# A four-layer attention and feed-forward kernel: a new order table, explicit waits for reused buffers, and a second buffer of reciprocal sums

## The reference, cut to what matters

```python
x = x + L0_xattn(ln(x), ctx, ctx)        # strict causal mask
x = x + ln(x) @ sign(W).T
x = x + L1_xattn(ln(x), ctx, ctx)        # causal mask
x = x + mixture(ln(x))                   # 16 experts, top 2, and 2 shared experts
x = x + L2_xattn(ctx, ln(x), mask)       # layer norms on q, k, v; a mask that is loaded
x = x + bitlinear_ffn(ln(x))             # 256 -> 1024 -> 256, weights rounded to -1, 0, 1
x = x + L3_xattn(ln(x), ctx, ctx)        # no weights, no mask
x = x + three_blocks(ln(x))              # low-rank corrected weights, layer norm, gelu
```

## Time and profile before

| | |
|---|---|
| median of 3 runs | 1159.62 us (1158.08 to 1163.7) |
| profiled execution, first to last instruction | 1166.1 us; the page gives no other time for it |
| PE, DVE, ACT, POOL busy | 90%, 78%, 69%, 48% |
| mean granted TensorE clock | 0.970 of full |
| moved by DMA | 140.03 MB, mean 120 GB/s |

### The profile page before, as it was taken

The page is one execution under the profiler, slowest core; times in us unless marked ns, Lnnn a source line. Parts: engine busy times, 40 slices in busy tenths (PEclk is TensorE's granted clock), DMA queues, the critical chain, the costliest instruction groups (busy, mean ns, idle before and its releaser), DMA issues.

```text
span 1166.1 us, 26103 instructions
## 1 busy us (share of the span) xinstructions
PE 1050.5 (90%) x8259; PEld 782.0 (67%) x8298; DVE 903.8 (78%) x3323; ACT 804.5 (69%) x1484; POOL 564.1 (48%) x1161
## 2 busy tenths in 40 slices
PE   7989999999999989898888898788898989989986
PEld 6667877777887866676666765556665665656664
DVE  3879887877564688898885588999997889887643
ACT  5757666566674555566565667656989899998962
POOL 7232364655122365577830125766455454545443
PEclk9999999999999998999999999979999999999997
DMA  7985322325667643412258864232132222222000
GB/s 239 312 284 143 92 74 56 91 74 173 203 181 210 200 127 82 136 47 84 81 185 262 249 184 147 84 92 76 39 100 73 73 55 56 83 64 55 1 19 19
DMA packets 102327, 140.03 MB, mean 120 GB/s; under 512 B 12336, under 2 KB 79792, under 8 KB 102192
## 3 DMA queue, kind: packets, MB, share of 16 engines
q1 hardware_dynamic: 98688, 129.57, 38.0%
q0 software_dynamic: 3072, 8.39, 2.3%
q10 hardware_dynamic: 432, 0.39, 0.1%
HBM read 65.43 MB, written 22.54 MB: 75 GB/s over the span
## 4 chain that ended last, share of the span: by engine, by line
PE 40%; DVE 18%; ACT 15%; DMA 8%; issue 7%; SPq 5%; POOL 5%; another core or an unknown queue 1%; DVEq 0%; POOLq 0%; ACTq 0%
PE ps L1559 9%; PE ps L1688 4%; ACT probs L2010 4%; PE ps L1580 4%; PE ps L1598 4%; SPq L2890 3%; PE ps L1781 3%; PE ps L1552 3%; PE ps L1566 2%; ACT q_st L2027 2%; DVE ps L2247 2%; DMA w<-in_expert 2%; PE ps L1601 2%; DVE ps L2255 2%; PE ps L1748 1%
## 5 line engine op out<-in xcount | busy, mean ns | idle before, releaser
L2010 ACT ACTIVATE probs<-ps 128x384 f32<-128x384 f32 (+1 forms) x512 | 260.2, 545 | 91.4 <-PE ps L1601 46.4
L1580 PE MATMUL ps<-k_st,q_st 96*128 96x256 bf16 (+1 forms) x1024 | 172.4, 266 | 26.8 <-DVE neg_max L2247 10.3
L1598 PE MATMUL ps<-q_st,k_st 104*128 104x256 bf16 (+1 forms) x1024 | 178.0, 263 | 16.8 <-ACT probs L2010 12.3
L2027 ACT ACTIVATE q_st<-ps 8x1024 bf16<-8x1024 f32 x128 | 129.9, 1016 | 24.4 <-PE ps L1669 21.8
L1580 PEld LDWEIGHTS ps<-k_st,q_st 96*128 96x128 bf16 x1024 | 86.8, 100 | 79.1 <-DVE neg_max L2247 19.1
L2247 DVE CUSTOM_DVE_ANT_0 ps<-ps,diag_s 128x128 f32<-128x128 f32 (+1 forms) x384 | 123.3, 358 | 20.9 <-PE ps L1580 18.7
L1598 PEld LDWEIGHTS ps<-q_st,k_st 104*128 104x128 bf16 x1024 | 90.7, 99 | 61.7 <-issue 19.5
L1688 PE MATMUL ps<-probs,v 128*32 128x256 f32 (+1 forms) x2048 | 126.0, 365 | 2.0 <-ACT probs L2010 1.9
L2576 POOL TENSOR_SCALAR var_eps<-mv 128x2 f32<-128x2 f32 (+1 forms) x115 | 27.8, 242 | 185.2 <-DVE mv L2139 180.1
L2255 DVE CUSTOM_DVE_ANT_0 ps<-ps,mask_s 128x256 f32<-128x256 f32 x256 | 101.4, 452 | 6.2 <-PE ps L1580 5.8
L2658 POOL CAST parts<-qf 128x512 bf16<-128x512 f32 x64 | 40.5, 633 | 100.3 <-DVE qf L2166 44.7
(11 more groups left out here) (275 smaller groups left out, 2548.9 us busy)
## 6 DMA issues: line engine op xcount, KB each, us to landing
k_st<-parts SPq DMA_DIRECT2D x192, 128.0 KB
q_st<-parts SPq DMA_DIRECT2D x189, 128.0 KB, 2.8
w<-in_expert SPq DMA_DIRECT2D x62, 384.0 KB, 4.2
x_rows<-wo SPq DMA_DIRECT2D x10, 768.0 KB, 10.9
ctx_t<-in_ctx_t SPq DMA_DIRECT2D x16, 256.0 KB, 3.0
ring<-x_rows SPq DMA_DIRECT2D x31, 128.0 KB, 3.3
y_rows<-ring SPq DMA_DIRECT2D x31, 128.0 KB, 3.7
xn_t<-x_rows SPq DMA_DIRECT2D x31, 128.0 KB, 4.0
```

The source lines that it names most:

```text
L1580: last = mm(t[:, c0:c0 + n], head(q_st, r, h, KROWS, j * P, P), head(k_st, r, h, KROWS, 0, n), start=j == 0 or not by_pe, stop=not by_pe, ...
L1598: last = mm(t[:, j * S:j * S + n], head(k_st, r, h, KALL, j * P, P), head(q_st, r, h, KALL, skip, n), start=j == 0 or L == 3, stop=L == 3, ...
L2010: nc.scalar.activation(probs[:, (hg % 2) * HPG + h4, 0:width], tile_of(key)[:, 0:width], ACT.Exp, scale=SCALE).then_inc(*tile_drained(key))
L2027: nc.scalar.activation(out, tile_of(key)[KROWS:KALL, 0:S].unsqueeze(1).to_broadcast([2 * HPG, HPG, S]), ACT.Copy).then_inc(*tile_drained(key))
```

## The change

1. `AT` has new times (in hundredths of a microsecond, read with `clock[0] = t / 100`), so all engines get another order. The set of steps, 5,036, is the same. `DRAIN`, `ORDER` and the lanes are untouched.
2. `sum_inv` gets a buffer for each of the two pairs of head groups.
3. Waits that the old order made true by itself are written out: in `projected`, `quantised_copy`, `down_copy` (ACT), `normalise` (DVE), `load_batch` and `tile_load` (SP).
4. `wait_score` is gone from POOL's `scatter` and `fetch`.

Where some steps stand in the two tables, counted in `exp` steps of the 512 that stand ahead of them: all 12 `fill`s, the loads of both first masks and the second layer's weights are issued before the key stack of slot 2 (before: six `fill`s); the last `scatter` of the first group comes after 202 exponents (before: 152) and the first expert tile after 208 (before: 160); the `fetch`es of the first group all come after 256 exponents (before: after 202 to 226), as do the last `scatter`s of the second group (before: after 277 to 283). 256 exponents are the first half. Between the last exponent of slot 15 and the first of slot 16 stand 24 of the 62 `tile_up`, 11 of the 16 `up`, 7 layer 2 `token` projections and all 16 first `fetch`es (before: none of these).

```diff
 AT = (
-    (287, 292, 303, 305, 322, 325, 339, 342, 370, 373, 386, 391, 416, 419, 432, 435, 456, 459, 470, 473, 496, 498, 509, 512,
...
     for t, n in sorted((t, n) for n, times in enumerate(AT) for t in times):
-        clock[0] = t / 10
+        clock[0] = t / 100
...
-        sum_inv = sb("sum_inv", [P, SJ, 2 * HPG])
+        sum_inv = sb("sum_inv", [P, 2, SJ, 2 * HPG])
...
                 def projected(L, b):
+                    n = SLOT[L, b] - 1
+                    while n >= 0 and ORDER[n][0] == 3:
+                        n -= 1
+                    if n >= 0:
+                        wait_filled(act, ("wo", *ORDER[n]))
                     drain(("op", L, b), o_t[:, :, :])
...
                 def quantised_copy(b):
+                    if b:
+                        for T in range((b - 1) * SJ, b * SJ):
+                            for c in range(2):
+                                wait_filled(act, ("hu", T, c))
...
                 def down_copy(T):
+                    if T >= SJ:
+                        wait_filled(act, ("hd", T - SJ))
...
+                    if SLOT[L, b]:
+                        wait_drained(dve, ("ot", *ORDER[SLOT[L, b] - 1], pair))
+                    inv = sum_inv[:, pair, :, :]
...
-                    V.reciprocal(sum_inv[:, :, :], t[:, :, :, DH]).then_inc(*inverted.step((L, b, pair)))
+                    V.reciprocal(inv, t[:, :, :, DH]).then_inc(*inverted.step((L, b, pair)))
...
-            def wait_score():
-
-                n = sum(10 * clock[0] > t for t in AT[0])
-                if n:
-                    L, b = ORDER[(n - 1) // H]
-                    wait_filled(pool, ("s", L, b, *divmod((n - 1) % H, HPG)))
...
             def load_batch(L, b):
-                if L == 0 and b >= 4:
-                    wait_filled(sp, ("v", 1, b - 4))
+                read = b - 4 if L == 0 else b + 4
+                if L == 0 and b >= 4 or L == 2 and b < 4:
+                    for what in ("k", "v"):
+                        for layer in range(2):
+                            wait_filled(sp, (what, layer, read))
                 if L == 2:
-                    if b < 4:
-                        wait_filled(sp, ("v", 1, b + 4))
-                    else:
+                    if b >= 4:
+                        for what in ("k", "v"):
+                            wait_filled(sp, (what, 2, b - 4))
                         sp.wait_ge(*part_rest.at(("k", 3, b - 4)))
...
                     if GT <= i < GT + RING:
-                        wait_filled(sp, ("logit", LAST))
-                        wait_filled(sp, ("ed", LAST))
+                        for b in (B - 2, LAST):
+                            wait_filled(sp, ("logit", b))
+                            wait_filled(sp, ("ed", b))
```

More of the change, by code:

```diff
@@ L107, in step, with drain @@
         return self.sem, self.unit
+    def drain(self, key):
+        return self.sem, self.unit
     def at(self, key):
@@ L1429, in tile_drained @@
             new_drain_at[key] = clock[0] + DRAIN
-            return drained[bank_of[key]].sem, 1
+            return drained[bank_of[key]].drain(key)
         def wait_filled(eng, key):
@@ L2280, in normalise @@
                     wait_filled(dve, key)
+                    if SLOT[L, b]:
+                        wait_drained(dve, ("ot", *ORDER[SLOT[L, b] - 1], pair))
+                    inv = sum_inv[:, pair, :, :]
                     t = tile_of(key).rearrange("p (a h e) -> p a h e", a=SJ, e=DPAD)
-                    V.reciprocal(sum_inv[:, :, :], t[:, :, :, DH]).then_inc(*inverted.step((L, b, pair)))
+                    V.reciprocal(inv, t[:, :, :, DH]).then_inc(*inverted.step((L, b, pair)))
                     dve.wait_ge(*inverted.at((L, b, pair)))
                     out = o_tok[:, r, :, pair * 2 * HPG * DH:(pair + 1) * 2 * HPG * DH].rearrange("p a (h d) -> p a h d", d=DH)
-                    V.tensor_tensor(out, t[:, :, :, 0:DH], sum_inv[:, :, :].unsqueeze(3).to_broadcast([P, SJ, 2 * HPG, DH]), ALU.mult).then_inc(
+                    V.tensor_tensor(out, t[:, :, :, 0:DH], inv.unsqueeze(3).to_broadcast([P, SJ, 2 * HPG, DH]), ALU.mult).then_inc(
                         *tile_drained(key))
@@ L2801, in scatter @@
                             pool.wait_ge(*filling.at(11))
-                    wait_score()
                     G.indirect_dma_start(x_rows[b // NB], bass.IndirectOffsetOnAxis(ap=dest[:, b * SJ + a, k:k + 1], axis=0),
```

## The result

The changed kernel took 1173.30 us (median of 5 runs, 1166.27 to 1175.36) against 1159.32 us for the kernel before: a ratio of 1.0099, 95% interval 1.0062 to 1.0136. On another chip, in `changed_again`, the ratio was 1.0097 (1.0062 to 1.0133). The forecast was 1134, so the sign was wrong.

The account below looks back on a forecast made before the run. PE was taken to set the time: 857 us of matmul work divided by the rate the order allows. Seven stretches summed to 1140.5 us, less a 6.5 us offset gave 1134, with 8 in 10 from 1097 to 1162.

Parts of the forecast that it names:

- That the order can gain: The old order was good where few transfers ran; a new order can gain where many do, 1134 us in all.
- S1: Stretch from the start to exponent 64: 128 us, bounds 120 and 136, with the late key stack mostly covered.
- S5: Stretch from exponent 336 to 512: 290.7 us of work at its old rate 0.821, 354 us.
- S6: The tail after exponent 512: 21.4 us of work at rate 0.49, 44 us, bounds 40 to 53.
- S2: Stretch from exponent 64 to 128: 79.3 us of work at rate 0.853, 93 us, bounds 93 and 101.
- S3: Exponents 128 to 256: attention part with 175.2 us of work at rate 0.787, 223 us, bounds 217 and 242.
- S4: Stretch up to exponent 336: 136.9 us of work at rate 0.73, 187.5 us, bounds 170 and 209.
- The gap: Between exponents 256 and 257: 60.2 us of work at rate 0.54, 111 us.
- Rival D: The gap between exponents 256 and 257 falls to the low clock, 171 us instead of 111; 1194 us, chance 0.12.
- The offset of 6.5 us: The old profiled span stood 6.5 us above the median; the same was subtracted from the new sum, giving 1134.
- The other edits at nothing: New waits on ACT, SP and DVE, second sum_inv and removed wait_score each priced at about 0 us.
- Rivals B and C: B: S4 at 0.804, the gap at 0.656, 1097 us, chance 0.19. C: every stretch keeps its old rate, 1152.5, 0.14.

Follow-up runs that it names:

- changed_again: The changed kernel itself, run again on another chip as a control: ratio 1.0097 to the kernel before.
- fills_late: The changed kernel with eight of the twelve fills moved on SP behind the key and query stacks of slot 2: ratio 1.0001 to the kernel before.
- key_split_late: The changed kernel with the projection, split and rounding steps of slot 3's keys moved by 15 us in the order: ratio 1.0031 to the kernel before.
- both_repairs: The changed kernel with the fills_late edit plus a separate buffer and semaphores for the scatters: 1148.4 us, ratio 0.9892 to the kernel before.
- all_fills_late: both_repairs with the last four fills and layer 2's weights moved later too: ratio 0.9974 to the kernel before.
- waits_old_order: The changed kernel with the order table of before, keeping all the other edits: ratio 0.9985 to the kernel before.

## Why the prediction was wrong

**That the order can gain: right, but not for this kernel.** With two repairs of a local kind the new order is 1.0 to 1.1% faster than the old. In the profiled execution of that kernel, its fastest, the terms come out at 133.0, 90.7, 216.7, 110.6, 180.6, 363.1 and 46.4 us: sum 1141.1, where the forecast had 1140.5. That the sums are so close is luck: S1, S5 and S6 are 5, 9 and 2 us over, the others 16 under. Its median, 1148.4, is still 14 us above the 1134. S2, the attention part of S3, and S4 ran somewhat above the rates that I took from rows, in the changed kernel too (0.875, 0.81 and 0.75).

**S1, 128 forecast, 147.7 measured: the step that failed.** I had the bytes right (20 MB ahead of the stack, some 15 us of delay) and then wrote "most of it is cover: slots 0 and 1 give PE and ACT work to about 65 us". I asked what PE and ACT had to do, and not what stood in ACT's list. One instruction that rewrites the buffer of the late stack came ahead of slot 1's exponents, so the cover was exactly what was blocked. `fills_late` and `key_split_late` show it from both sides: take the bytes away, or the place in the list, and slot 1 is back at 62 to 65 us instead of 77.8. This is 13 to 15 of the 19.7 us; S1 takes 133 to 135 us in the repaired kernels, and what the other 5 to 7 are is open. The row was there to be read: the same wait stood twice in the old trace, 3.7 us in all.

**The gap, 111 forecast, 120.2 measured.** I priced it with rates from elsewhere, and weighed only whether its matmuls would run at the low clock. Rival D's mechanism is in it, but small: the falls cost about 3 us, not 60. The result came out slower, as in D, but by another way: the gap's clock was 0.93, and no rival had the wait of S1. Two in-order waits of ACT for a just issued scatter were the larger part: without them the gap is 12.7 us shorter, while the clock kept up with the waits left in place gives 3.3. They had no term in the sum. The only sentence of the prediction on what waits for the scatters is "nothing on PE waits for POOL then"; the engine that waits for them is ACT, for a buffer. Without these waits the gap has 107.5 to 110.6 us, the 111 of the forecast.

**S5, 354 forecast, 363.1 measured**, and the same in `both_repairs`: a term sized by one rate (0.821) for a stretch that is now 290.7/363.1 = 0.80. No experiment took it apart. S6's 43.8 us met its 44.

**The offset of 6.5 us.** I carried the distance between the profiled execution and the median over to the new kernel. It belonged to one execution, and the new one's lay the other way, which is 15.3 us of the 39.3 of the miss; even without any offset the forecast would have been 1140.5, a gain. Over the runs of the kernel before beside `fills_late`, the time falls with the granted clock of the run, by 750 us per unit (correlation -0.66); for `both_repairs` by 810 (-0.92), for `changed_again` by 940 (-0.88). It is looser elsewhere (-0.41 in `all_fills_late`). The old profile had a clock of 0.970 where the median run beside `fills_late` has 0.976, which by that slope is 4.5 of the 6.5 us. The changed kernel's profile had 0.974 against a median of 0.968, so it lay on the other side.

**The other edits at nothing: right as a sum in the old order** (`waits_old_order`), not tested one by one, nor in the new order. Rivals B and C: S4 ran at 136.9/182.2 = 0.75, S3's attention part at 0.81 and the gap at 60.2/120.2 = 0.50, so neither. Of the new waits that I named, PE's 13.4 us for `o_t` is none of them: it came from the DMA behind ACT.

**What stays open:** what binds the 108 us that the gap keeps, S5's 9 us, 5 to 7 us of S1, and the wait ahead of `o_raw`.

## What to carry to other kernels

Where a transfer becomes late, look for every instruction that waits for it, the writers of its source buffer too, and then read what stands behind each of them in that engine's list: cover counts only if it is ahead. Price a removed or moved stall by the engine that is blocked, not by the engine that waits in the data's path. And before carrying a profiled execution's distance to the median over, look at its clock beside that of the other runs: most of that distance can be its own.

## What the runs showed of the hardware

A `fill` of 768 KB took 0.61 us to issue in the kernel before at 55.4 us, and 1.4 us on the mean with ten in a row in the changed one (13.77 us for ten); six stack DMAs behind those took 9.4 us where they had taken 3.8. While these were issued, from 50 to 60 us, the core's transfers moved 420 GB/s. From issue to landing a stack DMA took 2.9 us at the median in the changed kernel and 10.0 at the longest (2.8 and 7.6 before). The last of a group of four scatters landed 4.3 and 5.5 us after its issue began, with 211 to 382 GB/s moved in the microseconds around. PE's clock came down to 0.50 with 0.29 us of work in 13, and 40 extra matmuls in two waits lifted the granted clock of the 120 us around them from 0.94 to 0.99. Comparable runs of one kernel spread over 0.5 to 1.4%, and the time falls with the run's granted clock, with correlations from -0.41 to -0.95.
